# Two graph layers and two expert layers on one core: first query tile split during the edge count, spread by transpose, the last expert store moved to SyncE, a record load delayed

## The chip, the cores and the metric

The kernel runs on one core of a Trainium2 chip. The core has TensorE (PE in the profile, with its weight loads as PEld), VectorE (DVE), ScalarE (ACT), GpSimd (POOL) and SyncE (SP), each with its own instruction stream, and sixteen DMA engines that serve all of them. SyncE starts its transfers through hardware queues (q1, hardware_dynamic), GpSimd through software queues whose descriptors it writes itself (q0, software_dynamic). The metric is the time of one execution on the device in microseconds (us), the median of several runs; lower is better.

## The reference

A node array `x` of 1250 x 512 goes through four residual layers. What matters here:

```python
n, q, k, v = 1250, h @ Wq, h @ Wk, h @ Wv               # layer 1: graph attention, 8 heads of 64
e = einsum('ehd,ehd->eh', k[src], q[dst]) / 8           # 20000 edges
attn = segment_softmax(e, dst)
a = segment_sum(attn[:, :, None] * v[src], dst)         # then Wo, layer norms, a small MLP
x = x + layer1(layernorm(x))

x = x + of                                              # layer 2: 8 experts, top 2, capacity 187
#   h = gelu(x_e @ w1[e] + b1[e]) (512 -> 2048);  out = h @ w2[e] + b2[e];  scattered back by weight

x0, x1 = node_feats @ W_up                              # layer 3: messages over the same edges
tpw = silu_mlp(edge_attr_8) @ W_mlp4                    # per edge weights
msg = segment_sum(products of tpw, x0[src], x1[src], edge_attr_4)   # then W_out

x = x + shared_ffn + bank_sp + bank_fq                  # layer 4: two top-1 banks of 8 experts
```

## The kernel before

The whole array `X` stays in SBUF as 10 tiles of 125 nodes. The program is a sequence of blocks. Every block gives each engine a stream of its own, and all engines meet in a barrier at its end, so the last engine to arrive sets the start of the next block. The order within a block is written by hand, with semaphores; there is no scheduler. The blocks in the order of time, with the stretch of the profile:

- `front` (0 to 233 us): edge records are put in order, and q, k, v are computed. q goes to a DRAM tensor `q_dram`.
- `count_edges` (233 to 345 us): builds a dense table `LA` of logarithms of edge counts, node by node. VectorE writes one-hot tiles (`ohD`, line 564, a comparison with two SBUF inputs; `ohS`, line 569), TensorE multiplies them into a ring of four PSUM regions (line 588), ScalarE takes the logarithm of a finished region (line 619) and clears it (line 624). GpSimd does nothing but "grants": for each of 98 groups it loads a number and waits until that group's region is free (lines 537 to 539). SyncE loads the records and then writes zeros into the inputs of the later expert layers (line 1469).
- `attend` (345 to 665 us): for 10 tiles of queries and 8 heads each, TensorE computes scores against all 1250 keys (line 707, `scores`), VectorE adds the mask and takes the maximum (line 791), ScalarE exponentiates (line 852), TensorE transposes the probabilities (line 716, `turn`; 10 transposes for a head), VectorE and ScalarE copy them, and TensorE multiplies by V (line 725, `values`). There is one score buffer, so scores of head n+1 start after the mask of head n. A query tile must first be split in two parts, upper and rest: SyncE loads `QF` (line 671, `stage`), GpSimd copies it into `QS` (line 693) and subtracts (line 695), and then releases `q_split` (line 698), for which the scores of head 0 wait (line 707). Once per tile the inverse sums `rz_wide` (125 x 512) are spread over the output's layout by four products with the identity (line 736, `spread_inverse`), and VectorE multiplies by them (line 810).
- `dense`, `place_choices` (665 to 908 us): layer norms, MLP, routing of tokens to experts.
- `experts0` (908 to 1278 us): 8 experts one after the other. The rows of an expert (188 x 512) are turned back (line 1595) and copied by VectorE in two halves of 94 rows into `ye` (line 1677, counted by `back_moved`). GpSimd then stores both halves with one transfer of 94 x 2 x 512 (line 1562) and waits for it. `recycle` follows: GpSimd clears the used semaphores (line 100) between two barriers.
- `messages` (1278 to 1722 us) begins with `send_rows`: GpSimd gathers for each of 10 tiles the two expert rows of every node (line 1713, 20 gathers into a ring of 8 buffers `got`), VectorE adds them to `X` (line 1781, counted by `added`) and computes the moments; ScalarE normalises, TensorE transposes and multiplies, and SyncE stores the rows to `up_dram` (line 1707). Between the tiles (`between(t)`) VectorE does other preparations: it clears `MSG` (20 blocks, four at once, lines 1963 and 1967), converts the edge records (line 1970, from `t` = 4 on), scales weights, and builds the first one-hots. SyncE loads `RECS` (1568 KB of edge records, line 1839) and weights at the beginning of the block. When all rows are in `up_dram`, the loop over 196 tiles of edges begins.
- `tail`, `experts1` (1722 to 2015 us): layer 4.

The constants: `TILES` = 10, `BLOCKS` = 20, `GROUPS` = 98, `EXPERTS` = 8, `HALF0` = 94, `ROWS0` = 188.

## Time and profile before

| what | value |
|---|---|
| median of 3 runs | 2013.15 us (2009.31, 2013.15, 2964.96) |
| the profiled execution | 2016.69 us, span of the core 2015.0 us, mean granted clock 0.923 |
| busy: PE, PEld, DVE, ACT, POOL | 1669.8, 1204.0, 972.8, 727.3, 570.0 us |
| DMA | 262.15 MB, mean 130 GB/s |

The span is the time from the first to the last instruction of the core; the execution's own time has 1.7 us more. One of the three runs is far above the other two and is an outlier; the median is not touched by it. PE is busy for 83% of the span, but this is a mean over stages with different limits. The chain of waits that the profile prints ends with the last instruction and reaches back only to 1813.75 us, into layer 4; none of the changed places lies on it. So each place has to be read in its own stretch of time.

### The profile page before, as it was taken

To read this page: it belongs to the slowest core of one execution; us is meant where nothing else is said; L and a number is where in the kernel's file an instruction comes from. 1 tells how busy PE (TensorE), PEld (TensorE's weight loads), DVE (VectorE), ACT (ScalarE), POOL (GpSimd) and SP (SyncE) were. 2 spreads that over 40 slices of the span, in tenths; PEclk is the share of its full clock that TensorE was granted. 3 is DMA by queue.
4 is the path that set the end of the run, shared out by engine and by line. 5 is a ranking of instruction groups with operands and counts; after the bars stand their busy time and mean duration, and the time that the engine had idled before them with its cause. 6 is when DMAs were issued, how large, how long until landed. Compare 5 with 4: busy or idle time off the path is not lost. (4 is left out here: it accounts for less than half of the span.)

```text
span 2015.0 us, 33411 instructions
## 1 busy us (share of the span) xinstructions
PE 1669.8 (83%) x10239; PEld 1204.0 (60%) x10240; DVE 972.8 (48%) x1983; ACT 727.3 (36%) x1707; POOL 570.0 (28%) x656
## 2 busy tenths in 40 slices
PE   1990165999999697897999999179999999898992
PEld 1540032788888465557999999155555555646661
DVE  9210297666666475340000000358888888441232
ACT  1220053555555233441122211145555555422330
POOL 4777400110110121240000000435555554133132
PEclk9995599899999897897999999559999999998996
DMA  6200360110100601546777650545555555539983
GB/s 171 58 7 6 134 253 10 31 22 11 20 10 1 152 2 64 191 142 215 241 227 227 191 178 9 131 135 167 155 156 157 155 154 142 199 91 326 289 247 128
DMA packets 140526, 262.15 MB, mean 130 GB/s; under 512 B 41715, under 2 KB 59479, under 8 KB 135961
## 3 DMA queue, kind: packets, MB, share of 16 engines
q1 hardware_dynamic: 92792, 175.23, 27.8%
q0 software_dynamic: 47648, 85.82, 15.0%
q8 instruction: 50, 0.82, 0.2%
q14 instruction: 36, 0.29, 0.1%
HBM read 203.48 MB, written 57.38 MB: 129 GB/s over the span
## 5 line engine op out<-in xcount | busy, mean ns | idle before, releaser
L1891 PE MATMUL acc<-prod,ohy 128*64 128x256 f32 x1176 | 276.9, 385 | 8.3 <-DVE prod L2004 8.2
L1936 ACT ACTIVATE ohy<-oh,RECS 128x64 f32<-128x64 f32 x784 | 208.1, 336 | 168.6 <-PE acc L1891 168.6
L1891 PEld LDWEIGHTS acc<-prod,ohy 128*64 128x64 f32 x1176 | 153.8, 137 | 147.8 <-issue 83.3
L1868 POOL DMA_INDIRECT rows<-up_dram,idx x196 | 185.7, 947 | 172.3 <-DVE prod L2004 144.4
L1894 PE MATMUL acc<-prod,ohy 128*64 128x256 f32 x784 | 200.8, 394 | 0.0
L2004 DVE TENSOR_TENSOR prod<-w_ps,rows 128x768 f32<-128x768 f32 x196 | 185.7, 947 | 0.0
L244 POOL DMA_INDIRECT rec_dram<-recs,pos x157 | 154.5, 984 | 69.8 <-issue 48.9
L1672 DVE TENSOR_SCALAR FT<-y_ps,b2T 128x188 f32<-128x188 f32 x32 | 13.2, 413 | 328.8 <-PE y_ps L1621 328.8
L1609 PE MATMUL hid_ps<-FT,W 128*128 128x188 f32 x1024 | 168.5, 326 | 0.7 <-ACT FT L1646 0.7
L588 PE MATMUL ps<-ohS,ohD 128*128 128x512 f16 (+1 forms) x392 | 70.0, 305 | 118.6 <-DVE ohS L569 115.5
L1609 PEld LDWEIGHTS hid_ps<-FT,W 128*128 128x128 f32 x1024 | 166.1, 193 | 0.9 <-issue 0.9
L1621 PE MATMUL y_ps<-hid,W 128*128 128x188 f32 x1024 | 164.5, 323 | 0.0
L1621 PEld LDWEIGHTS y_ps<-hid,W 128*128 128x128 f32 x1024 | 162.9, 190 | 0.0
L791 DVE CUSTOM_DVE_ANT_0 S<-score_ps,LA 125x1250 f32<-125x1250 f32 x80 | 116.7, 1459 | 87.2 <-PE score_ps L707 86.3
L852 ACT ACTIVATE S<-S,mx 125x1250 f32<-125x1250 f32 x80 | 107.2, 1340 | 127.4 <-DVE mx L796 127.4
L588 PEld LDWEIGHTS ps<-ohS,ohD 128*128 128x128 f16 x392 | 33.8, 99 | 155.3 <-issue 151.2
L707 PE MATMUL score_ps<-KT,QS 128*125 128x512 f32 (+1 forms) x480 | 113.8, 373 | 12.3 <-POOLq L698 10.6
L2003 DVE TENSOR_TENSOR prod<-w_ps,rows 128x256 f32<-128x256 f32 x196 | 82.3, 420 | 70.4 <-PE acc L1891 54.0
L1562 POOL DMA_DIRECT2D yout<-ye x8 | 13.5, 1690 | 355.4 <-DVE ye L1677 355.4
L1884 PE MATMUL w_ps<-W,h 64*128 64x512 f32 x392 | 111.1, 644 | 0.0
L716 PE MATMUL turn_ps<-ident,S 125*125 125x125 f32 x800 | 108.4, 283 | 1.3 <-ACT PT L857 1.2
L725 PE MATMUL out_ps<-PT,V 125*64 125x125 f32 x1600 | 103.0, 274 | 1.5
(373 smaller groups left out, 2725.3 us busy)
## 6 DMA issues: line engine op xcount, KB each, us to landing
W<-in_L_ffn_w SPq DMA_DIRECT2D x16, 4096.0 KB, 23.4
bankW_sp<-in_L_ffn_W_sp SPq DMA_DIRECT2D x2, 4096.0 KB, 24.6
xin<-zeros SPq DMA_DIRECT2D x31, 256.0 KB
h_dram<-h3e SPq DMA_DIRECT2D x24, 256.0 KB, 4.5
h<-h_dram SPq DMA_DIRECT2D x24, 256.0 KB, 2.7
QF<-q_dram SPq DMA_DIRECT2D x20, 250.0 KB, 4.3
xin_sp<-zeros SPq DMA_DIRECT2D x18, 256.0 KB
xin_fq<-zeros SPq DMA_DIRECT2D x18, 256.0 KB
```

The lines of the kernel that those rows point to most:

```text
L244: pool.indirect_dma_start(out=rec_dram, out_offset=bass.IndirectOffsetOnAxis(ap=pos[0:rows_of, c:c + 1], axis=0), in_=recs[0:rows_of, c, : ...
L707: last = nc.tensor.matmul(score_ps[:P, c0:c0 + cn], QS[par][:, part, h, 0:P], KT[:, h, c0:c0 + cn], start=part == 0, stop=part == 1)
L716: last = nc.tensor.transpose(turn_ps[:P, 128 * s:128 * s + P], S[:, h % 2, P * s:P * (s + 1)], ident[:P, :P])
L791: nc.vector.tensor_tensor_reduce(out=S[:, h % 2, :], in0=score_ps[:P, 0:NODES], in1=LA[:, 2 * pairs - 2 + par, :], scale=1.0, scalar=-3e38 ...
L1609: last = nc.tensor.matmul(hid_ps[:, m % 4, 0:ROWS0], W1[b][:, k, 128 * m:128 * (m + 1)], xT[:, k, :], start=k == 0, stop=k == KC - 1)
L1621: last = nc.tensor.matmul(y_ps[:, d % 2, 0:ROWS0], W2[b][:, m, 128 * d:128 * (d + 1)], hid[:, m, :], start=m == 0, stop=m == MC0 - 1)
L1868: pool.indirect_dma_start(out=rows[:, t, :], out_offset=None, in_=up_dram, in_offset=bass.IndirectOffsetOnAxis(ap=idx[:, par, t:t + 1], ax ...
L1884: last = nc.tensor.matmul(w_ps[:, 2 * (pair % 2) + half, :], h3[mine, par, 128 * pair:128 * (pair + 1)], W4[mine, :], start=True, stop=True)
L1891: upper = lambda m: nc.tensor.matmul(acc[0:HALFB, bank, :].rearrange("p (b c) -> p b c", c=MUL)[:, m:4:3 - m, :], ohs[:, 1 + m, :], pr[:, ...
L1894: lower = lambda q: nc.tensor.matmul(acc[HALFB:128, bank, 256 * q:256 * (q + 1)], ohs[:, 0, :], pr[:, 0:3:2, :] if q == 0 else pr[:, 3:5, ...
L1936: last = nc.scalar.activation(ohy[:, t % OHY, i, :], oh[:, par, t, :], ACT.Copy, scale=RECS[:, bass.ds(BATCH * g + t, 1), 4 + i])
L2004: nc.vector.tensor_tensor(pr[:, 2:8, :].rearrange("p (a m) c -> p a m c", a=2), w[:, 2:4, :].unsqueeze(2).to_broadcast([128, 2, 3, MUL]), ...
```

## The change

Four edits, in four places.

1. **Query tiles.** `QF`, `QS`, their semaphores and the two programs `stage` (SyncE) and `split` (GpSimd) move out of `attend` into a new function `query_tiles`, called ahead of `count_edges`. SyncE loads query tile 0 behind the record load of `count_edges`, and GpSimd splits it after its last grant. `attend` starts with tile 1 on both engines. What each tile waits for is otherwise unchanged.
2. **Spreading the inverse sums.** The four products with the identity become four transposes.
3. **Last expert's store.** Expert 7's rows are no longer stored by GpSimd but by SyncE, in two halves of 94 x 512, each as soon as VectorE has copied it; SyncE waits for both. GpSimd stores experts 0 to 6 as before.
4. **Records.** SyncE loads `RECS`, the message weights and the first hidden chunks only after the first tile of `X` has got its two expert rows. VectorE clears 12 blocks of `MSG` before the first tile and 4 blocks after each of the tiles 0 and 1, instead of 4 before and 4 after each of the tiles 0 to 3.

```diff
+        def query_tiles(stack):
...
+            def stage(sp, i):
+                if not isinstance(i, int) or i > 0:
+                    sp.wait_ge(upper_ready, 2 * i)
+                    sp.sem_inc(tick, 1)
+                for half in range(2):
+                    sp.dma_start(QF[DK * half:DK * (half + 1)], q_dram[:, :, bass.ds(i * P, P)]).then_inc(q_loaded, 16)
+
+            def split(pool, i, par):
+                pool.wait_ge(q_loaded, 32 * (i + 1))
+                if not isinstance(i, int):
+                    pool.wait_ge(tiles_scored, i - 1)
+                    pool.sem_inc(tick, 1)
+                nc.gpsimd.tensor_copy(QS[par][:, 0, :, 0:P], QF[:]).then_inc(upper_ready, 1)
+                pool.wait_ge(upper_ready, 2 * i + 1)
+                nc.gpsimd.tensor_tensor(QS[par][:, 1, :, 0:P], QF[:], QS[par][:, 0, :, 0:P].bitcast(F32),
+                                        ALU.subtract).then_inc(upper_ready, 1)
+                pool.wait_ge(upper_ready, 2 * i + 2)
+                pool.sem_inc(q_split[par], 1)
...
                         sp.dma_start(RECS[:], rec_dram.rearrange("(p c) w -> p c w", p=128)).then_inc(loaded, 16)
-
+                        stage(sp, 0)
                         zeros_in = fill_zeros(sp, xin0, zeroed)
...
                         groups(pool, grant)
+                        split(pool, 0, 0)
...
-                        sp.sem_inc(upper_ready, 1)
-                        for par in range(2):
-                            stage(par, par)
-                        with sp.Fori(0, TILES // 2 - 1) as r:
+                        stage(sp, 1)
+                        with sp.Fori(1, TILES // 2) as r:
                             for par in range(2):
-
-                                stage(2 * r + 2 + par, par)
+                                stage(sp, 2 * r + par)
...
-                                last = nc.tensor.matmul(out_ps[:, 1 - par, P * q:P * (q + 1)],
-                                                        rz_wide[:, 2 * q:2 * q + 2, :].rearrange("p h c -> p (h c)"),
-                                                        ident[:P, :P], start=True, stop=True)
+                                last = nc.tensor.transpose(out_ps[:, 1 - par, P * q:P * (q + 1)],
+                                                           rz_wide[:, 2 * q:2 * q + 2, :].rearrange("p h c -> p (h c)"),
+                                                           ident[:P, :P])
...
+                        last = EXPERTS - 1
+                        for c in range(2):
+                            sp.wait_ge(back_moved, 2 * last + c + 3)
+                            sp.dma_start(yout0[last * ROWS0 + HALF0 * c:last * ROWS0 + HALF0 * (c + 1), :],
+                                         ye[last % 2][:, c, :]).then_inc(last_stored, 16)
+                        sp.wait_ge(last_stored, 32)
...
-                        with pool.Fori(0, EXPERTS // 2) as r:
+                        with pool.Fori(0, EXPERTS // 2 - 1) as r:
                             for b in range(2):
...
+                                store(r, b)
+                        store(EXPERTS // 2 - 1, 0)
...
+            def first_added(sp):
+                sp.wait_ge(added, per_tile)
...
                         load_mix(sp)
+                        first_added(sp)
                         sp.dma_start(RECS[:], rec_dram.rearrange("(p c) w -> p c w", p=128)).then_inc(recs_loaded, 16)
...
-                        CLEAR = 4
+                        CLEAR, FIRST = 4, 12
+                        nc.vector.memset(MSG[:, 0:FIRST, :], 0.0)
                         nc.vector.memset(acc[:], 0.0)
-                        nc.vector.memset(MSG[:, 0:CLEAR, :], 0.0)
 
                         def between(t):
-                            if t < BLOCKS // CLEAR - 1:
-                                nc.vector.memset(MSG[:, CLEAR * (t + 1):CLEAR * (t + 2), :], 0.0).then_inc(cleared, 1)
+                            if t < (BLOCKS - FIRST) // CLEAR:
+                                nc.vector.memset(MSG[:, FIRST + CLEAR * t:FIRST + CLEAR * (t + 1), :], 0.0).then_inc(cleared, 1)
```

How the instructions stand on GpSimd at the end of `count_edges` and the start of `attend`. The loads of `turnI` are the last grants, and `QS` is the split query tile. Before:

```order
L537 TENSOR_LOAD turnI
L537 ISA x2
L537 TENSOR_LOAD turnI
L537 ISA x2
L520 UNCONDITIONAL_BRANCH
L682 UNCONDITIONAL_BRANCH
L686 UNCONDITIONAL_BRANCH
L686 ISA
L693 CAST QS<-QF 128x8x125
L694 REGISTER_ALU
L695 TENSOR_TENSOR QS<-QF,QS 128x8x125
```

After the change:

```order
L566 TENSOR_LOAD turnI
L566 ISA x2
L566 TENSOR_LOAD turnI
L566 ISA x2
L514 CAST QS<-QF 128x8x125
L516 TENSOR_TENSOR QS<-QF,QS 128x8x125
L549 UNCONDITIONAL_BRANCH
L697 UNCONDITIONAL_BRANCH
L514 CAST QS<-QF 128x8x125
L516 TENSOR_TENSOR QS<-QF,QS 128x8x125
```

The first split stands ahead of the block's end (the branch of line 549), right behind the last grant; the second split is the first work of `attend`.

How they stand on SyncE at the end of `experts0` and the start of `messages`. Before:

```order
L1544 COMPARE_AND_BRANCH
L1525 UNCONDITIONAL_BRANCH
L1836 UNCONDITIONAL_BRANCH
L1701 DMA Wup<-in_L_gnn_W_up 128x128
L1702 DMA Wup<-in_L_gnn_W_up 128x128
L1839 DMA RECS<-rec_dram 128x3136
L1841 DMA W<-in_L_gnn_W_mlp 64x512 x2
```

After the change:

```order
L1549 COMPARE_AND_BRANCH
L1562 DMA yout<-ye 94x512 x2
L1530 UNCONDITIONAL_BRANCH
L1854 UNCONDITIONAL_BRANCH
L1716 DMA Wup<-in_L_gnn_W_up 128x128
L1717 DMA Wup<-in_L_gnn_W_up 128x128
L1858 DMA RECS<-rec_dram 128x3136
L1860 DMA W<-in_L_gnn_W_mlp 64x512 x2
```

The two half stores are the last work of SyncE in `experts0`. The record load keeps its place in the row, but a wait now stands between it and the loads of `Wup`.

On VectorE at the start of `messages`, before:

```order
L1962 MEMSET acc 128x1024
L1963 MEMSET MSG 128x2048
L1781 SCALAR_TENSOR_TENSOR X<-got,weight,X 125x512 x2
L1785 BN_STATS st_2<-X 125x6
L1786 BN_AGGR mv<-st_2 125x2
L1967 MEMSET MSG 128x2048
```

After the change:

```order
L1981 MEMSET MSG 128x6144
L1982 MEMSET acc 128x1024
L1799 SCALAR_TENSOR_TENSOR X<-got,weight,X 125x512 x2
L1803 BN_STATS st_2<-X 125x6
L1804 BN_AGGR mv<-st_2 125x2
L1986 MEMSET MSG 128x2048
```

The clear ahead of the first rows is three times as long, and two of the four clears between the tiles are gone further down.

## Rows read from the trace of the kernel before

**Rows 1.** Timeline: start us, us, engine, line, instruction [idle before <- releaser], count to attend
```profile
345.27 18.36 SPq L671 DMA_DIRECT2D QF<-q_dram  x6
350.42 1.02 POOL L693 CAST QS<-QF 128x1000 fp32r<-128x1000 f32 x1 [116.62 <-DMA QF<-q_dram]
351.53 2.12 POOL L695 TENSOR_TENSOR QS<-QF,QS 128x1000 fp32r<-128x1000 f32 x1
...
353.76 2.47 PE L707 MATMUL score_ps<-KT,QS 128*125 128x512 f32 x6 [10.57 <-POOLq L698]
...
357.94 2.47 PE L707 MATMUL score_ps<-KT,QS 128*125 128x512 f32 x6 [1.71 <-DVE mx L791]
```
**Rows 2.** Windows: us, busy (x) of PE, PEld, DVE, ACT, POOL, PEclk, DMA share, GB/s
```profile
305.00:325.00 20.00, 14.67 (x85) 7.06 (x84) 19.53 (x64) 10.34 (x13) 0.00 (x0) 1.00 0.00 0
...
346.00:347.00 1.00, 0.00 (x0) 0.00 (x0) 0.63 (x1) 0.42 (x1) 0.00 (x0) 0.83 0.28 38
...
366.00:372.00 6.00, 5.08 (x43) 4.24 (x43) 3.92 (x7) 4.22 (x6) 0.00 (x0) 1.00 0.04 6
```
**Rows 3.** One line, the grants: ns min/median/max, first and last start us
```profile
L539 POOLq EVENT_SEMAPHORE  x98: 17/17/17, 234.4 to 330.0; - x98
```
**Rows 4.** Timeline of place_choices: the GpSimd cast beside DVE L1347
```profile
797.19 2.26 POOL L1320 CAST ohT<-zeros 40x2500 fp32r<-40x2500 f32 x1
```
**Rows 5.** One line, DVE L1347: ns min/median/max of its two instructions
```profile
L1347 DVE TENSOR_TENSOR oh<-count,idxF x2: 243/1242/2242, 797.3 to 799.6; 125x80 f32<-125x80 f32 x2
```
**Rows 6.** Timeline of attend at the end of a tile: TensorE
```profile
397.75 0.97 PEld L736 LDWEIGHTS out_ps<-ident,rz_wide 125*128 125x128 f32 x8 [0.17 <-issue]
...
398.64 1.17 PEld L716 LDWEIGHTS turn_ps<-ident,S 125*125 125x125 f32 x10
...
399.76 1.37 PE L707 MATMUL score_ps<-KT,QS 128*125 128x512 f32 x6
```
**Rows 7.** Timeline: end of experts0, start of messages and its first tiles
```profile
1262.22 1.28 DVE L1677 COPY ye<-turn_ps 94x512 f32<-94x512 f32 x2 [0.73 <-PE turn_ps L1595]
1264.38 1.67 POOL L1562 DMA_DIRECT2D yout<-ye  x1 [38.18 <-DVE ye L1677]
...
1279.59 0.42 SPq L1839 DMA_DIRECT2D RECS<-rec_dram  x1
1279.74 1.28 POOL L1713 DMA_INDIRECT got<-yout,slot_out  x1 [0.82 <-issue]
...
1280.33 1.76 DVE L1963 MEMSET MSG<- 128x2048 f32 x1 [0.42 <-issue]
...
1293.74 0.75 DVE L1781 SCALAR_TENSOR_TENSOR X<-got,weight,X 125x512 f32<-125x512 f32 x1 [1.30 <-DMA got<-yout,slot_out]
...
1297.72 1.61 DVE L1781 SCALAR_TENSOR_TENSOR X<-got,weight,X 125x512 f32<-125x512 f32 x2
...
1302.55 1.60 DVE L1781 SCALAR_TENSOR_TENSOR X<-got,weight,X 125x512 f32<-125x512 f32 x2
...
1322.56 1.61 DVE L1781 SCALAR_TENSOR_TENSOR X<-got,weight,X 125x512 f32<-125x512 f32 x2
...
1326.14 1.60 DVE L1781 SCALAR_TENSOR_TENSOR X<-got,weight,X 125x512 f32<-125x512 f32 x2
```
**Rows 8.** Windows while the last expert's rows are stored, columns as in Rows 2
```profile
1272.00:1273.00 1.00, 0.00 (x0) 0.00 (x0) 0.00 (x0) 0.00 (x0) 0.00 (x0) 0.50 0.12 49
...
1276.00:1277.00 1.00, 0.00 (x0) 0.00 (x0) 0.00 (x0) 0.00 (x0) 0.00 (x0) 0.50 0.00 0
```
**Rows 9.** Timeline: a SyncE transfer of 94 x 2 x 512 and who waits for it
```profile
908.75 1.10 SPq L1528 DMA_DIRECT2D xe<-xin  x2
...
918.66 1.51 PE L1584 MATMUL turn_ps<-ident,xe 94*128 94x94 f32 x8 [9.16 <-DMA xe<-xin]
```
**Rows 10.** Timeline of layer 4: a first gather with no record load beside it
```profile
1979.63 1.25 POOL L2453 DMA_INDIRECT xe<-yout_fq,slots  x1 [2.67 <-DMA yout_fq<-FT]
...
1985.20 0.75 DVE L2564 SCALAR_TENSOR_TENSOR X<-xe,top_of,X 125x512 f32<-125x512 f32 x1 [9.08 <-DMA xe<-yout_fq,slots]
```

More of the change, by code:

```diff
@@ L492, in turning, with count_edges @@
             return pe_part, act_part
-        def count_edges(LA):
+        def query_tiles(stack):
+            sb = tile_in(stack)
+            QF = sb("QF", [128, HEADS, P])
+            QS = [sb(f"QS{par}", [128, 2, HEADS, 128], F32R) for par in range(2)]
+            q_loaded, upper_ready, tiles_scored, tick = sems_in(stack)("q_loaded", "q_upper_ready", "tiles_scored", "query_tick")
+            q_split = sems_in(stack)("q_split0", "q_split1")
+            def stage(sp, i):
[15 more added lines that the diff above has]
+                pool.sem_inc(q_split[par], 1)
+            return QS, tiles_scored, q_split, stage, split
+        def count_edges(LA, stage, split):
             HALFN = NODES // 2
@@ L625, in _, with attend @@
                                                      ACT.Copy).then_inc(evicted, 1)
-        def attend(KT, V, LA, T):
+        def attend(KT, V, LA, T, QS, tiles_scored, q_split, stage, split):
             with ExitStack() as st:
@@ L634, in attend @@
                 spread, lifted, deepened = sems_in(st)("inverse_spread", "values_lifted", "mask_deepened")
-                QF = sb("QF", [128, HEADS, P])
-                QS = [sb(f"QS{par}", [128, 2, HEADS, 128], F32R) for par in range(2)]
-                q_loaded, upper_ready, tiles_scored = sems_in(st)("q_loaded", "q_upper_ready", "tiles_scored")
-                q_split = sems_in(st)("q_split0", "q_split1")
                 S = sb("S", [P, 2, NODES])
@@ L665, in _ @@
                     def _(sp):
[L666 to L677 removed]
+                        stage(sp, 1)
+                        with sp.Fori(1, TILES // 2) as r:
                             for par in range(2):
[L680 removed]
+                                stage(sp, 2 * r + par)
                     @block.gpsimd
                     def _(pool):
[L685 to L686 removed]
+                        split(pool, 1, 1)
+                        with pool.Fori(1, TILES // 2) as r:
                             for par in range(2):
[L688 to L698 removed]
+                                split(pool, 2 * r + par, par)
                     @block.tensor
@@ L1510, in experts0 @@
                 stored = sems_in(st)("stored0", "stored1")
+                (last_stored,) = sems_in(st)("last_stored")
                 (b_turned, b_ready, x_turned, x_moved, hid_done, hid_moved, y_done, y_moved, back_done,
@@ L1791, in on_dve @@
                                                        in1=rstd[:, t:t + 1], op0=ALU.mult, op1=ALU.mult).then_inc(scaled, 1)
-            return load, store, fetch, all_stored, on_pe, on_act, on_dve
+            return load, first_added, store, fetch, all_stored, on_pe, on_act, on_dve
         def messages(MSG, picks):
@@ L2601, in gnn_moe_gnn_moe @@
             LA = sb1("LA", [P, TILES, NODES])
-            count_edges(LA)
-            attend(KT, V, LA, FT)
+            QS, tiles_scored, q_split, stage, split = query_tiles(attention)
+            count_edges(LA, stage, split)
+            attend(KT, V, LA, FT, QS, tiles_scored, q_split, stage, split)
         with ExitStack() as moe:
```

34 lines of the change are left out of this document (9 added, 25 removed).

## The prediction

> **What bounds the kernel now.** The page's chain of waits covers only the last 200 us, in layer 4, which the change leaves alone. I therefore read the timeline at each of the four places, and the windows for TensorE's granted clock. The question at each place is which event ends the wait last.
>
> At the start of attention it is the query tile. All engines come out of the barrier by 345.27, when SyncE issues the load of `QF`; GpSimd copies (1.02 us) and subtracts until 353.65; TensorE starts at 353.76 and had been idle for 10.57 us [rows 1]. In that gap its clock fell from full (2.4 GHz) to half (1.2 GHz): the mean of 346 to 347 is 0.83 [rows 2]. So the first scores take 2.47 us [rows 1] where a later head's take 1.37 [rows 6]. In the middle of attention TensorE goes from one group of matmuls to the next with gaps of 0.17 us at most [rows 6]: it is the bound there. In the count it is VectorE, busy 19.53 of 20 us, with TensorE at 14.67 [rows 2].
>
> At the end of the experts it is one transfer: VectorE is done at 1263.50, GpSimd issues at 1264.38 and needs 1.67 us for that [rows 7], and the data move at 49 GB/s until just before 1276.1, with a DMA share of 0.12 of sixteen engines, so two of them [rows 8]. At the start of `messages` it is the first gathers: issued at 1279.74, just after the 1568 KB record load of 1279.59; the second sum of tile 0 starts only at 1293.74 [rows 7].
>
> **Part 1, query tile 0.** Its load and split leave the start of attention. Load: two transfers behind the record load; the zero fills behind them are over by 305 (DMA share 0.00 [rows 2]) and the count lasts until 345, so the delay of these fills costs nothing. The split: the last grant is at 330.0 [rows 3], so GpSimd splits from 330.1 to 333.3, long before the barrier. TensorE can then start at about 345.3: **8.5 us** earlier, if the count ends as before.
>
> It won't quite. GpSimd computes beside VectorE here for the first time. A VectorE comparison with two SBUF inputs took 2.242 us while a GpSimd cast of 2.26 us ran, and its twin right after it 0.243 [rows 4, 5]: it waited for the cast. `ohD` is such a comparison. `ohS` has one SBUF input, and I don't know whether it waits too. GpSimd holds on for 1.02 + 2.12 = 3.14 us [rows 1]. If both kinds wait, VectorE, which has no slack, loses 3.1 us; if the two `ohS` of a group (about 0.3 us each, from 19.53 us over 64 instructions [rows 2]) run on beside each of the two GpSimd instructions, 3.1 - 2 x 0.6 = 1.9; if nothing waits, 0. I take 2.6, between the first two, since the instruction of rows 5 is the very kind of `ohD`. The Trainium skill (SBUF — State Buffer, "Who interferes with whom") says the same as a rule: a VectorE instruction with two SBUF inputs and a GpSimd instruction that reads SBUF exclude each other for their whole length; by it `ohD` waits and a one-port `ohS` does not, which would make the loss 1.9. By that rule, the trace agrees for `ohD`. Gain of the start: 8.5 - 2.6 = **5.9**.
>
> The clock: TensorE's pause becomes 2 us, and in the old trace the clock was still full 3 us after TensorE's last work (it fell inside 346 to 347). So attention should start at full clock. The first heads form a chain, because there is one score buffer: scores, mask, scores; the second scores came 4.18 us after the first [rows 1], of which 2.47 - 1.37 = 1.1 us was the half clock. Two such steps and a bit, as clock is full from 366 on [rows 2]: **2.3 us**. Tile 1 is now loaded at 345.3 and split by 353.7; it is wanted only 8 heads later, more than 20 us: nothing.
>
> **Part 2, transposes.** The four products stand as 8 passes and take 398.64 - 397.75 = 0.89 us; ten transposes of the same 125 x 125 take 399.76 - 398.64 = 1.12, 0.11 each [rows 6]. Four then take 0.45. TensorE is the bound, so 0.44 x 10 tiles = **4.5 us**. The bound from below is 2.0: on some tiles the next copy of ScalarE may be what TensorE then waits for.
>
> **Part 3, last store.** The first half can be issued at 1262.95 and the second at 1263.6, instead of both at 1264.38 by GpSimd. The nearest row for SyncE's part is the load of the same 94 x 2 x 512 to `xe`, issued at 908.75 and there at 918.66 [rows 9]: 9.9 us, no quicker than GpSimd's 11.7 (1264.38 to 1276.1) but for the issue. So half sizes don't halve the time: I let both together take 9.9 us from the first issue, and they land at 1272.8 instead of 1276.1, **3.3 us** earlier. By the Trainium skill (DMA: Bandwidth & Descriptors, "Why a DMA increments its semaphore by 16 and not by 1") the number of engines is the largest divisor up to 16 of the outer sizes, so 94 rows get two, and SyncE's transfers use the lowest ones; both halves would then share the same two, which is what I assumed. If they use different ones, 4 us more are gained. GpSimd also reaches the barrier early and settles there while the store runs, for which I add 0.7: **4.0**. Bounds: 2.5 and 8.
>
> **Part 4, records.** Without the load of 1568 KB beside them, gathers land as in layer 4, where the first took 1979.63 to 1985.20, 5.6 us [rows 10]. A first gather issued at 1279.74 lands at 1285.3; the second, issued after 1.28 us of GpSimd's work [rows 7] and a short gap, at about 1287.4 with a little more queueing, instead of 1293.74: **6.3 us**. Ahead of them VectorE now clears three times 2048 columns at 1.76 us each [rows 7] and `acc` (half a clear's columns, so 0.9 us), from 1279.0 to 1285.2: hidden by the first gather, at the edge. A tile with a clear takes 1302.55 - 1297.72 = 4.83 us, one without 1326.14 - 1322.56 = 3.58 [rows 7]; two tiles lose their clear: **2.5 us**. The records are issued when the second sum is done, about 1288, take some 8 us and are wanted by tile 4, about 1304 on this scale. They now collide with the gathers of tiles 2 and 3; a gather beside the records took up to 14 us from issue (1279.74 to 1293.74 spans two), but these have 8 to 10 us. I take off 0.5: **8.3**. Bounds: 2.5 (tiles 2 and 3 wait for what tile 0 waited for) and 8.8. GpSimd's 20 gathers, 1.28 us [rows 7] and a gap each, so about 1.5, end by 1310, ahead of tile 9 at 1320.
>
> **Sum.** 5.9 + 2.3 + 4.5 + 4.0 + 8.3 = 25.0 us. Span 2015.0 - 25.0 = 1990.0, that execution 1991.7. It was 3.5 us above the median of the runs, so the median becomes 2013.15 - 25.0 = **1988 us**, 1.2% less. A measurement of this kernel can tell about 2% (40 us) from no change, so this would be within.
>
> **Rivals.**
> - *The parts are worth less (12 in 100).* Each is hidden or eaten by the next wait: part 1 at 8.5 - 3.1 = 5.4 with no clock gain, part 2 at 2.0, part 3 at 2.5, part 4 at 2.5. Sum 12.4, time 2001. For it: the tight places named above, in part 4 above all. Against it: they'd all have to fall out badly.
> - *VectorE isn't held up and the half stores run side by side (15 in 100).* 8.5 + 2.3 + 4.5 + 8 + 8.8 = 32.1, time 1981. Against the first half stands rows 5.
> - *Slower: transposes let the clock fall (3 in 100).* If transposes don't count as work for the clock and attention fell to half clock, TensorE's time for a tile would grow by nearly its own length, about 8 x 3.6 = 29 us. One tile eats the whole gain, so from two tiles on it's slower: 1988 + 2 x 29 = 2046. The Trainium skill (TensorE: Matmul & The Clock Gate, "Part 4: PE-mode transpose") has that rule. Against it: ten transposes already stand in every head and the clock is 1.00 [rows 2]; the change adds 0.45 us of them to a tile of 29 and takes away 0.89 of matmuls.
> - *The change doesn't do what it says (5 in 100):* the grants are late or the load of tile 0 lands late and TensorE starts at 353 as before: 25.0 - 8.2 = 16.8, time 1996. Against it: fifteen us lie between the last grant and the barrier.
>
> The forecast itself has 65 in 100, with 1983 to 1994. The whole range reaches from 1977, the second rival less 4 us for the runs' spread (2009.31 against 2013.15), to 2002, the first rival. Faster by over 2% would need 40 us, more than all upper bounds together: 0.01. Slower by over 2%: the clock rival: 0.03.
>
> **What would show it.** Part 1: a GpSimd copy of `QF` at about 330; there, single `ohD` of 1 to 2 us instead of 0.4, the last `ohS` 2 to 3 us later, then first scores of 1.4 us within 3 us of the last count matmul. Part 2: 4 instead of 8 passes per tile, and a tile 0.44 us shorter. Part 3: two SyncE transfers at 1263 (shifted by the parts above), landing about 9 us later, and 12 us from VectorE's last copy to the first gather instead of 16. Part 4: second sum 8 us after the first gather's issue instead of 14, tiles 2 and 3 at 3.6 us, no wait for the records. I'm wrong if tiles 2 to 4 wait for gathers or records, or if the end of the count moves by less than 1 us or more than 4.

## The result, and the profile after

The changed kernel takes 1991.8 us, median of 4 runs (1988.5 to 1993.5); the kernel before took 2011.8 beside it, or 2010.4 without the outlier of 2965 us that is one of its 4 runs. The ratio is 0.9895 (95% interval 0.9883 to 0.9908): 1.05% or some 20 us less, clear of the noise but within the 2% that count as no change. The profiled spans are 2015.0 and 1991.8 us. The prediction said 1988, range 1977 to 2002. The time lies in the range, but the gain is some 20 us and not 25.

To compare places I count every trace from the start of the count block (GpSimd's first instruction there): what lies ahead of it is unchanged. `before`, `after`, `before_again`, `spread_by_matmul` and `fill_and_last_rows` ran on chips that reach the count after 233 us (kernel before: 2012 to 2015 us). The others ran on two chips, one for each of their sets, that reach it 76 to 89 us later and take 5 to 9 us more in the loop of `messages` (kernel before: 2105 and 2103 us); I call them the late chips. The columns are the starts of the first scores and of the last value product, the end of VectorE's last copy in `experts0`, the starts of the first gather and of the first index copy in `messages`, and the end of the program; the last three columns are differences.

| kernel | scores | values | last copy | gather | idx | end | values - scores | gather - copy | idx - gather |
|---|---|---|---|---|---|---|---|---|---|
| before | 120.7 | 430.2 | 1030.4 | 1046.7 | 1110.4 | 1781.9 | 309.5 | 16.2 | 63.7 |
| before_again | 121.0 | 430.0 | 1027.5 | 1043.8 | 1107.7 | 1776.9 | 309.0 | 16.2 | 64.0 |
| after | 113.8 | 418.9 | 1018.6 | 1031.0 | 1091.4 | 1758.9 | 305.1 | 12.4 | 60.3 |
| after_again | 114.1 | 417.8 | 1016.7 | 1029.1 | 1090.0 | 1764.8 | 303.7 | 12.4 | 60.9 |
| queries_as_before | 121.3 | 425.7 | 1022.9 | 1035.3 | 1096.1 | 1771.6 | 304.4 | 12.4 | 60.7 |
| spread_by_matmul | 114.5 | 422.5 | 1025.6 | 1038.0 | 1097.8 | 1765.6 | 308.0 | 12.4 | 59.8 |
| split_at_head | 120.6 | 425.5 | 1021.1 | 1033.5 | 1094.8 | 1770.8 | 304.9 | 12.4 | 61.3 |
| split_on_vector | 112.3 | 416.1 | 1016.0 | 1028.5 | 1089.4 | 1766.0 | 303.9 | 12.4 | 60.9 |
| records_late | 113.7 | 417.5 | 1018.8 | 1031.3 | 1091.0 | 1767.9 | 303.9 | 12.4 | 59.7 |
| records_early | 113.7 | 417.7 | 1019.1 | 1031.6 | 1086.9 | 1766.2 | 303.9 | 12.4 | 55.3 |
| store_80_14 | 113.9 | 418.2 | 1015.2 | 1020.7 | 1080.7 | 1756.6 | 304.3 | 5.5 | 60.0 |
| all_three | 112.5 | 417.4 | 1018.7 | 1024.3 | 1079.4 | 1752.7 | 304.9 | 5.6 | 55.1 |
| fill_and_last_rows | 112.9 | 416.1 | 1013.6 | 1019.2 | 1072.5 | 1745.2 | 303.2 | 5.5 | 53.4 |

By places the change gives 6.9 us at the first scores, 4.4 to 5.3 in the attention, 3.8 at the store and 3.1 to 3.4 in the first part of `messages`: 18 to 19 together.

**The count and the start of attention.** Timeline of the changed kernel while GpSimd splits the first query tile beside VectorE's one-hots, and at the first scores:

```profile
328.47 1.44 DVE L599 TENSOR_SCALAR ohS<-nodes,halfS 128x625 f16<-128x625 f16 x2
328.64 1.09 POOL L514 CAST QS<-QF 128x1000 fp32r<-128x1000 f32 x1 [94.94 <-issue]
329.81 2.41 POOL L516 TENSOR_TENSOR QS<-QF,QS 128x1000 fp32r<-128x1000 f32 x1
329.83 0.41 DVE L594 TENSOR_TENSOR ohD<-nodes,key 128x256 f16<-128x256 f16 x1
330.16 2.54 DVE L599 TENSOR_SCALAR ohS<-nodes,halfS 128x625 f16<-128x625 f16 x2
...
332.95 0.66 DVE L599 TENSOR_SCALAR ohS<-nodes,halfS 128x625 f16<-128x625 f16 x2
333.18 1.13 PE L618 MATMUL ps<-ohS,ohD 128*128 128x512 f16 x3 [1.55 <-DVE ohS L599]
...
346.77 2.44 PE L711 MATMUL score_ps<-KT,QS 128*125 128x512 f32 x6 [2.16 <-PEq L549]
```

A pair of `ohS` takes 0.66 us, and 1.44 and 2.54 beside the two GpSimd instructions: 2.66 us lost. I call this the hold-up. The 10.57 us pause of [rows 1] is 2.16, yet the first scores take 2.44 us, at half clock. Windows of the changed kernel (columns as in [rows 2]) show two falls:

```profile
333.50:336.00 2.50, 2.10 (x9) 0.88 (x8) 2.50 (x9) 0.00 (x0) 0.00 (x0) 0.50 0.00 0
337.00:346.00 9.00, 5.82 (x36) 2.81 (x34) 5.82 (x20) 1.33 (x2) 0.00 (x0) 1.00 0.00 0
347.00:356.00 9.00, 7.29 (x24) 6.15 (x25) 4.88 (x8) 2.99 (x4) 3.16 (x2) 0.50 0.28 58
```

**Attention.** `rz` is made once a tile, so its first and last start give nine tiles: 268.4 us in the kernel before, 263.9 after, 0.50 us a tile. TensorE's line has 40 instead of 80 passes. First the kernel before, then the changed one, one tile name (count, ns min/median/max, first to last start):

```profile
L834 DVE RECIPROCAL rz<-z x10: 193/193/193, 391.8 to 660.2; 125x8 f32<-125x8 f32 x10
```
```profile
L838 DVE RECIPROCAL rz<-z x10: 191/193/193, 384.9 to 648.8; 125x8 f32<-125x8 f32 x10
L740 PE MATMUL out_ps<-ident,rz_wide x40: 270/270/326, 390.9 to 652.4; 125*128 125x125 f32 x40
```

**The last store and the first sums.** Timeline of the changed kernel, to compare with [rows 7]:

```profile
1250.29 1.28 DVE L1692 COPY ye<-turn_ps 94x512 f32<-94x512 f32 x2 [0.73 <-PE turn_ps L1610]
1251.01 0.87 SPq L1562 DMA_DIRECT2D yout<-ye  x2
...
1263.99 1.29 POOL L1731 DMA_INDIRECT got<-yout,slot_out  x1 [0.82 <-issue]
1264.31 5.18 DVE L1981 MEMSET MSG<- 128x6144 f32 x1 [12.73 <-issue]
...
1270.52 1.53 DVE L1799 SCALAR_TENSOR_TENSOR X<-got,weight,X 125x512 f32<-125x512 f32 x2
...
1283.33 0.75 DVE L1799 SCALAR_TENSOR_TENSOR X<-got,weight,X 125x512 f32<-125x512 f32 x1 [3.14 <-DMA got<-yout,slot_out]
1285.13 0.75 DVE L1799 SCALAR_TENSOR_TENSOR X<-got,weight,X 125x512 f32<-125x512 f32 x1 [1.05 <-DMA got<-yout,slot_out]
...
1290.79 0.75 DVE L1799 SCALAR_TENSOR_TENSOR X<-got,weight,X 125x512 f32<-125x512 f32 x1 [2.38 <-DMA got<-yout,slot_out]
```

The sums are the `SCALAR_TENSOR_TENSOR`, two for each tile. The second one of tile 0 starts some 7.3 us behind the first gather's issue, not 14.0, and no longer waits for a gather but for the clears. Then tiles 2 and 3 wait 3.14, 1.05 and 2.38 us for their gathers. While the two halves of the store run, the DMA engines move as little as in [rows 8]:

```profile
1256.00:1257.00 1.00, 0.00 (x0) 0.00 (x0) 0.00 (x0) 0.00 (x0) 0.00 (x0) 0.50 0.13 51
```

So the data take as long as before. In windows of 1 us the engines are busy from 1266 to 1276 in the kernel before and from 1251 to 1261 in the changed one, some 9 us in both; VectorE's last copy ended at 1263.50 and at 1251.57. What the change saved is the time between that copy and the data.

### The profile page after: what moved, and what is told of

Read it like the earlier page. It is cut to its first block and busy times, and to the rows that moved or that the text cites. A ratio compares the mean times of both kernels' runs of the same rounds, so it can differ in the third digit from the quotient of the medians.

```text
span 1991.8 us, 33311 instructions
## 1 busy us (share of the span) xinstructions
PE 1664.9 (84%) x10199; PEld 1197.0 (60%) x10200; DVE 975.4 (49%) x1981; ACT 726.3 (36%) x1707; POOL 569.2 (29%) x655
## 5 line engine op out<-in xcount | busy, mean ns | idle before, releaser
L720 PEld LDWEIGHTS turn_ps<-ident,S 125*125 125x125 f32 x800 | 94.4, 190 | 13.0 <-issue 11.2
```

The source lines that it names most:

```text
L720: last = nc.tensor.transpose(turn_ps[:P, 128 * s:128 * s + P], S[:, h % 2, P * s:P * (s + 1)], ident[:P, :P])
```

## The experiments

Each is the changed kernel with an edit, timed in 4 to 6 executions beside the kernel before, in three sets. `after_again` is the changed kernel itself, and `before_again` is the kernel before, in a single execution.

**queries_as_before**: the query code of the kernel before, the rest of the change kept.

> Undoes the first part alone: queries are loaded and split in the attention block as in the kernel before, the other three parts stay. My account: the three parts give 4.9 (transposes), 3.8 (store) and 3.3 us (records), 12.0 together, and the first part is worth 7. So this one lies 12 to 13.5 us below the kernel before and 7 above the changed kernel. If the parts lean on each other (an earlier start of the attention that is lost at a later wait, so that undoing it costs nothing), it lies as low as the changed kernel, 20 below. If the account is short of something that the traces don't show (their spans differ by 23), it lies 16 below.

Ratio 0.9921 (0.9900 to 0.9941), 15 us below the kernel before. First scores at 121.3, 7.2 behind `after_again`, where the kernel before has them; by the places the part is worth 7.2 us. The totals can't settle it: the changed kernel itself, in the next set and on another of the late chips, also had 0.9921, and the two intervals are 9 and 12 us wide. Behind the first scores the long pause costs nothing: values - scores is 304.4 here and 303.7 to 305.1 in the eight kernels that have the transposes and the short one.

**split_at_head**: the first split ahead of the count's grants.

```diff
+                        stage(sp, 0)
                         sp.dma_start(RECS[:], ...).then_inc(loaded, 16)
-                        stage(sp, 0)
...
+                        split(pool, 0, 0)
                         groups(pool, grant)
-                        split(pool, 0, 0)
```

> The changed kernel, with the first queries loaded ahead of the count's records and split by GpSimd ahead of the first grant, while VectorE still waits for the records (its first one-hot in the changed kernel starts at 241.36, 8.4 us after the block's start). Theory 1, the hold-up: in the changed kernel the two one-hots L599 beside the split took 1.44 and 2.54 instead of 0.66, together 2.65 us; here none of the last one-hots is longer than 0.7, and the first scores, which stood 113.8 us behind the start of the count, stand 111.1 to 111.5 behind it. Theory 2, the clock: TensorE's clock was half at 333.1 to 336.5, when the late one-hots left it gaps of 1.9 us, and half again at 346.7 to 357.0. If the second fall comes of the first gaps, both are gone here and the first score group takes 1.2 instead of 2.44 us, for 2 us more. Rival: the pause of 2.1 us between the blocks brings it down by itself, the first group still takes 2.4, and only the 2.6 come. Rival 2: the split now delays the first grants, the one-hots start up to 3 us later, and the gain is eaten. By theory 1 alone 2.6 us below the changed kernel (22.6 below the kernel before), with theory 2 another 2 to 2.3; by rival 2 no difference to the changed kernel.

Ratio 0.9941 (0.9921 to 0.9961). This is 13 us below the kernel before, where 20 (rival 2) to 25 were expected. No `ohS` is over 0.39 us, so the hold-up is gone with GpSimd's work beside it; but rival 2 holds, and more than it said: the last one-hot ends 116.3 us behind the start (109.8 to 110.6 with the change) and the scores come at 120.6. The clock's first fall, beside the hold-up, is gone, and the one at the first scores is not (they take 2.44 us): theory 2 fails. The records, now loaded second, let the first one-hot start 12.6 instead of 10.7 us behind the start, which is 1.9 of it. The grants, one line of this kernel, start 9.7 us behind the block's start (at 318.2) instead of 1.3 and take 94.5 us from the first to the last, as in the other traces (94.2 to 95.6):

```profile
L568 POOLq EVENT_SEMAPHORE  x98: 17/17/17, 327.9 to 422.4; - x98
...
  DVE ohD L594: 7.6, 20
```

VectorE waits for them 20 times, 7.6 us. GpSimd's head start over VectorE was slack that the count uses up.

**split_on_vector**: VectorE splits, behind its last one-hot.

```diff
-                        split(pool, 0, 0)
...
                         groups(dve, one_hots)
+                        split(dve, 0, 0, nc.vector)
```

> The changed kernel, with the first queries' cast and subtraction done by VectorE behind its last one-hot, not by GpSimd beside the last one-hots. Theory, the hold-up: VectorE is idle from its last one-hot (342.8) to the start of the attention (346.7), 3.9 us; a cast and a subtraction of 1000 columns take it 1 us each, so they are hidden behind the last count matmuls and the last logarithms; the one-hots L599 take 0.66 us throughout; last one-hot and first scores come 2.6 us sooner, 111.2 us behind the start of the count. The run before this one, split_at_head, moved the split ahead of GpSimd's grants and lost 6.4 us, since the grants of 0.97 us each then set the pace; here the grants keep their place. Clock: if the gaps of TensorE beside the hold-up are what brought its clock down at 346.7, the first score group takes 1.2 us instead of 2.44 and another 2 come; if the 2.1 us pause does, it still takes 2.4. Rival: the grants (last at 328.5 in the changed kernel) bind the last groups, the one-hots end at the same time with shorter instructions and longer waits, and nothing is gained; or VectorE's split is longer than 3.9 us and the scores wait for it. By the theory 2.6 us below the changed kernel, or 4.6 with the clock; by the rivals 0 or slower.

```profile
429.27 0.67 DVE L514 CAST QS<-QF 128x1000 fp32r<-128x1000 f32 x1
429.98 1.20 DVE L516 TENSOR_TENSOR QS<-QF,QS 128x1000 fp32r<-128x1000 f32 x1
...
433.70 1.93 PE L711 MATMUL score_ps<-KT,QS 128*125 128x512 f32 x6 [2.13 <-PEq L549]
```

This timeline shows the split over at 431.2, 2.5 us ahead of the first scores. The last one-hot ends at 107.9, 2.7 ahead of `after_again` (110.6); the first scores gain 1.8 of it (114.1 to 112.3). So the hold-up cost the end of the one-hots what it measured. With no gap of TensorE beside it the first fall of the clock is gone (1.00 in every microsecond of the last 20 ahead of the scores), the second is not: the gaps of the hold-up aren't what brings it. The time of the first scores (1.93 us here) is no sign of it, since in `after_again`, with the hold-up, they take 1.39 and the clock falls only 1.6 us behind their start. The ratio, 0.9923 (0.9897 to 0.9948), is that of `after_again`: 2 us are below what so few executions resolve.

**spread_by_matmul**: the transposes of part 2 back to products (`nc.tensor.matmul(..., start=True, stop=True)`).

> Undoes the second part alone: the four products with the identity (32-bit, two passes each) in place of the transposes. If my account holds, a tile of the attention takes 30.3 us instead of 29.8 and the last values come 4.5 to 5 us later behind the first scores (303.8 to 305.1 in the changed kernel, 309.5 in the kernel before); the kernel lies 4.5 to 5 us above the changed kernel, 11 to 15 below the kernel before. Rival: the spread is hidden beside VectorE and ScalarE and the shorter attention of the changed kernel comes of the earlier start: 0.

Ratio 0.9923 (0.9907 to 0.9938), 16 us below the kernel before, where the changed kernel was 20 below it on a like chip. Nine tiles take 268.3 us again (the line of `rz`, as above), 4.5 more than with the transposes. values - scores is 308.0, against 305.1 in the changed kernel's first trace and 303.7 in its second: 2.9 and 4.3 us. The account holds.

```profile
L838 DVE RECIPROCAL rz<-z x10: 194/194/194, 384.6 to 652.9; 125x8 f32<-125x8 f32 x10
```

**store_80_14**: each of the last two stores cut at row 80.

```diff
-                            sp.dma_start(yout0[last * ROWS0 + HALF0 * c:..., :], ye[last % 2][:, c, :]).then_inc(last_stored, 16)
-                        sp.wait_ge(last_stored, 32)
+                            for p0, p1 in ((0, 80), (80, HALF0)):
+                                sp.dma_start(yout0[last * ROWS0 + HALF0 * c + p0:..., :], ye[last % 2][p0:p1, c, :]).then_inc(last_stored, 16)
+                        sp.wait_ge(last_stored, 64)
```

> The changed kernel, with each of the last two stores (94 rows, outer size 94 = 2 x 47, seen on two DMA engines at some 50 GB/s, 10.1 us from the first issue to landing) cut in two, of 80 and of 14 rows. Theory, the number of engines follows the outer size: 80 rows go over 16 engines and 14 over 14, the rows land within 3 to 4 us of the first issue, and the first gather comes 6 to 7 us sooner after the last copy (12.4 us in the changed kernel, 5.5 to 6.5 here). Rival: the split by rows is no matter and a store of so many rows stays at two engines: same 10 us. Rival 2: four issues of some 0.6 us each on SyncE and their four landings cost what the engines bring: 2 to 3 us gained. By the theory 6.5 us below the changed kernel (26.5 below the kernel before), by the rivals 0 or 2.5.

Ratio 0.9878 (0.9858 to 0.9899), 27 us below the kernel before. The changed kernel had 15.8 in its own set. Timeline and two windows:

```profile
1323.36 1.28 DVE L1693 COPY ye<-turn_ps 94x512 f32<-94x512 f32 x2 [0.73 <-PE turn_ps L1611]
1324.08 1.68 SPq L1563 DMA_DIRECT2D yout<-ye  x4
...
1330.17 1.29 POOL L1732 DMA_INDIRECT got<-yout,slot_out  x1 [0.82 <-issue]
```
```profile
1326.00:1327.00 1.00, 0.00 (x0) 0.00 (x0) 0.00 (x0) 0.00 (x0) 0.00 (x0) 1.00 0.52 152
1327.00:1328.00 1.00, 0.00 (x0) 0.00 (x0) 0.00 (x0) 0.00 (x0) 0.00 (x0) 1.00 0.00 0
```

In the last microsecond of the stores the DMA engines move 152 GB/s instead of 51, and in the one before it 219 at a share of 0.78 instead of 0.13 (0.95 in its busiest half). All is over by 1327, and it is 5.5 us from the last copy to the first gather instead of 12.4: the theory's 6.9 us, in every kernel that has this edit. More transfers alone don't do it: the change's two halves stayed at 0.13.

**records_late**: records asked for after tile 2's sums, used after tile 6.

```diff
-                sp.wait_ge(added, per_tile)
+                sp.wait_ge(added, 3 * per_tile)
...
-                            elif t == BLOCKS // CLEAR - 1:
+                            elif t == BLOCKS // CLEAR + 1:
```

> The changed kernel, with the records asked for after the sums of tile 2 (not tile 0) and put to use after tile 6 (not tile 4), the two steps behind them after tiles 7 and 8. Theory, the collision moved: in the changed kernel the records' 1568 KB ran from 1273 to 1281.3 beside the gathers of tiles 2 and 3, whose sums waited 3.14, 1.05 and 2.38 us, and the gain of 6.7 us at tile 0's sum was 3.3 from tile 4 on. Here the first three waits shrink to 1 us or less together, later tiles have their gathers four tiles ahead and don't wait, and the tail of this stage is 3.4 us earlier relative to its first gather (up to 6 if all of the 6.6 us of waits are the records' doing). Rival: the gathers alone are that slow (20 of 1.3 us each on GpSimd's side), the waits stay, and the time is that of the changed kernel. Rival 2: the waits move on to the tiles whose gathers now meet the records, or the records are late at tile 6, and the stage ends within 1 us of the changed kernel's. By the theory 3.4 us below the changed kernel (23.4 below the kernel before), by the rivals 0 to 1.

Ratio 0.9901 (0.9879 to 0.9922), 20 us below the kernel before, where the theory wanted 23. By the places rival 2 holds: idx - gather is 59.7 (60.3 and 60.9 in the changed kernel), tiles 2 and 3 don't wait any more, tiles 5 to 7 do. The waits of VectorE in this stretch (total, times, longest us), first here, then in the changed kernel:

```profile
DVE X L1799 <- DMA got<-yout,slot_out: 6.5, 5, 2.3
```
```profile
DVE X L1799 <- DMA got<-yout,slot_out: 6.6, 3, 3.1
```

**records_early**: records loaded in the middle of the last expert, into columns of `FT` that nobody uses then.

```diff
+                        sp.wait_ge(hid_done, MC0 * last + MC0 // 2)
+                        sp.dma_start(RECS, rec_dram.rearrange("(p c) w -> p c w", p=128)).then_inc(records_in, 16)
...
-                        sp.dma_start(RECS[:], ...).then_inc(recs_loaded, 16)
```

> The changed kernel, with the message stage's records (1568 KB) loaded in the middle of the last expert, when the DMA engines move 0 to 8 GB/s, into a part of FT that nothing uses till the tail. In the two kernels with the load inside the stage (after tile 0's sum, after tile 2's sum) the sums waited 6.6 and 6.5 us for gathers, of tiles 2 and 3 in the one, of tiles 5 to 7 in the other. Theory, the bytes: the load takes its place from the gathers wherever it is in the stage; out of the stage it costs nothing, the waits fall to 2 us or less, and the copy of the indices comes 4.5 to 6.5 us sooner behind the first gather (60.3 us in the changed kernel, so 54 to 56). Rival: gathers and stores of rows (7.5 MB) are the bound by themselves, the waits stay with W4's and the hidden rows' loads, 0 to 1.5 us gained. Rival 2: the load in the last expert delays its weights or its last stores, 1 to 8 us lost there. By the theory 5.5 us below the changed kernel.

```profile
DVE X L1806 <- DMA got<-yout,slot_out: 1.4, 1, 1.4
```

The waits fall from 6.6 to 1.4 us and idx - gather from 60.9 (`after_again`) to 55.3: 5.5 us, as the theory of bytes has it. At both places inside the stage that were tried the load costs them. Ratio 0.9903 (0.9877 to 0.9929), 2 us below the changed kernel in its set, where 5.5 were due; the profiled execution lost 2.6 us between the last values and the last copy. Rival 2, that the load delays the last expert, isn't the reason: from the copy that ends the expert before to its own last copy it takes 39.9 us in all thirteen traces, and the gather follows the last copy by 12.4 as in `after_again`. The 2.6 us lie in unchanged code ahead of it.

**after_again**, the changed kernel on a late chip, and **before_again**.

> The changed kernel itself, beside which the other three of this set are read on the same chip. The count block and the attention stand as before: first scores 113.8 us behind the start of the count, first gather 12.4 us behind VectorE's last copy, first gather to the copy of the indices 60.3 us. If the difference to the kernel before is a matter of the chip, it is not 20 us here.

Ratio 0.9921 (0.9891 to 0.9950), 15.8 us.

> The kernel before, profiled once beside the others, since on this chip the changed kernel was 15.8 us (0.5 to 1.1%) below it and not 20 us (1.05%). Counted from the start of the count block, on the first chip: first scores 120.7, first gather of the messages 1046.7, first copy of indices 1110.4, last 1465.9, end 1781.5. If the account by places holds here too, the first scores stand 6.6 us, the first gather 17.5 us and the first copy of indices 20.3 us behind the changed kernel's (114.1, 1029.1, 1090.0). If the four parts are worth less on this chip, these differences are smaller; if what is missing lies in unchanged code behind them, the differences are these and the loop of messages or the tail differs.

It ran on a chip of the first kind, so it can't answer what the late ones do. But it gives the two kernels twice: first scores 120.7 and 121.0 against 113.8 and 114.1, gather - copy 16.2 twice against 12.4 twice, idx - gather 63.7 and 64.0 against 60.3 and 60.9. Parts 3 and 4 rest on these pairs, since neither was undone by itself. The stretch from the last values to the last copy, unchanged in all, takes 595.6 to 603.0 us over these thirteen traces, in no order with the edits: so single spans can't be compared closer than some 4 us either way, and the places can.

**all_three**: `split_on_vector`, `store_80_14` and `records_early` in one.

> The changed kernel with three edits at once: the first split on VectorE behind the last one-hot, the last stores cut in 80 and 14 rows, the records loaded in the last expert. Store alone was seen with 5.5 us from the last copy to the first gather (12.4 in the changed kernel). If the places don't lean on each other, the sum is 2.6 + 6.9 + 5.5 = 15 us below the changed kernel, 35 below the kernel before. If the earlier gathers only meet something else (the records land beside the stores, or the rows' way through the stage is bound by bytes), it is 9.5 to 12.

Ratio 0.9856 (0.9828 to 0.9884), 2074.7 against 2087.5 us: 12.8 less. By places: 1.6 at the scores, 6.9 at the store, 5.8 in `messages`, 14.3 together. The gains add up at the places, and the total has nearly all of them.

**fill_and_last_rows**: `all_three` with seven idle matmuls behind the count, and the last store of `up_dram` cut in 112 and 13 rows.

```diff
+                        pe.wait_ge(logged, 2 * (BLOCKS - 3))
+                        for _ in range(7):
+                            nc.tensor.matmul(ps[:, 0:512], ohD[:, 0, :], ohS[:, 0, 0:512], ...)
...
+                    for p0, p1 in ((0, 112), (112, P)) if t == TILES - 1 else ((0, P),):
```

> The kernel all_three with two edits at places far apart. First: seven matmuls of 512 columns on leftover one-hots fill most of the 2.13 us that TensorE idles between the last count matmul and the first scores; their sums are overwritten, nothing reads them. In all ten traces the granted clock goes to half 0 to 2 us behind the first scores (or ahead, in the kernels before with the longer pause) and stays there 6 to 10 us, also where VectorE was never held up. Theory 1, the pause does it: with the filling the clock stays 1.00 over the first 20 us of the attention, the first score group takes 1.2 to 1.4 us, and the last values come 1 to 3 us sooner behind the first scores (305 us in all_three). Theory 2, the attention's own gaps at its start (TensorE waits 0.8 to 1.7 us between its first groups) do it: the clock still falls some us behind the first scores, and 0 to 1 us is gained. Second: the last of the ten stores of 125 rows to up_dram, outer size 125 = 25 x 5, is cut in 112 and 13 rows. By the rule that the number of engines follows the outer size, 16 and 13 engines take it in place of 5, and the copy of the indices follows the last row's eviction by 2.5 to 3 us instead of 4.3. Rival: the 4.3 us are latency and the sums of tiles 8 and 9's stores, 0 gained. Together 1.5 to 4.5 us below all_three, 30 to 33 below the kernel before (28.6 for all_three on this chip).

**1979.1 us, ratio 0.9822 (0.9806 to 0.9837)**: 1.8% or 36 us below the kernel before, and the fastest of all by its median. 30 to 33 us were expected. The places give 3.0 of the 7.6 us below `all_three`, which ran on a late chip; the rest is not accounted for. Timeline and windows:

```profile
343.93 1.67 PE L635 MATMUL ps<-ohS,ohD 128*128 128x512 f16 x7
...
346.24 1.38 PE L715 MATMUL score_ps<-KT,QS 128*125 128x512 f32 x6 [0.64 <-PEq L549]
```
```profile
346.24:349.24 3.00, 1.38 (x6) 1.00 (x6) 2.75 (x3) 1.09 (x1) 0.00 (x0) 1.00 0.59 122
351.00:353.00 2.00, 2.00 (x11) 1.91 (x10) 1.12 (x1) 0.00 (x0) 1.62 (x2) 0.53 0.00 0
355.00:360.00 5.00, 3.67 (x26) 3.30 (x26) 3.70 (x6) 2.91 (x4) 0.00 (x0) 1.00 0.52 102
```

By windows of 1 us the clock falls 3.2 us behind the first scores and is back 6.6 behind them; in `all_three` it falls 0.4 us ahead of them and is back 9.8 behind. values - scores is 303.2 against 304.9. So filling most of the pause (0.64 us of it are left) doesn't keep the clock up, as theory 1 wanted. That leaves theory 2, the spaced first heads, as the likelier one; no run changed their spacing, so it isn't shown. What the filling gained is open too: the changed kernel alone showed half clock for 10.2 us in one trace and 6.8 in the other, with 305.1 and 303.7, so 1.7 us is hardly more than that spread. The cut store is plain. In the timelines of `all_three` and then of this kernel the copy of the indices comes 4.29 us behind the last eviction's end (1395.76 + 0.60) and then 2.62:

```profile
1395.76 0.60 ACT L1791 ACTIVATE out_rows<-up_ps 125x512 f32<-125x512 f32 x1 [2.16 <-PE up_ps L1761]
1400.65 0.19 POOL L1885 COPY idx<-srcI 128x8 int32 x1 [22.62 <-DMA up_dram<-out_rows]
```
```profile
1302.70 0.60 ACT L1796 ACTIVATE out_rows<-up_ps 125x512 f32<-125x512 f32 x1 [2.16 <-PE up_ps L1766]
1305.92 0.19 POOL L1890 COPY idx<-srcI 128x8 int32 x1 [20.96 <-DMA up_dram<-out_rows]
```

## Why the prediction was right, and where it was not

**Part 1, start: 5.9 said, 6.9 found.** The pause shrank by 8.4 us (8.5 said) and the hold-up was 2.66 (2.6 said). The one-hots' end came only 1.9 later: they began 0.8 us later, behind a later landing of the records, but VectorE's waits for grants and free regions in the count were 1.3 us shorter (3.9 instead of 5.2). Neither was in my working, and the last count matmul ended only 1.5 later, which makes 8.4 - 1.5 = 6.9. *Who* waits was wrong: I bet on `ohD`, and `ohS` it was. So it is in part luck that 2.6 came out. In each pair one `ohS` lasts until just behind the end of the GpSimd instruction (329.73 and 332.22): 1.14 and 2.24 us, to 0.01, in all six traces with the split at this place. `ohD`, which came in between, took its usual 0.41 us, and GpSimd's subtraction beside it 2.41 us instead of 2.14, in all six too. So it looks as if each side waits for the other's instruction, whoever is first; that `ohD` is what stretches the subtraction was not tried by itself. The Trainium skill (SBUF — State Buffer, "Who interferes with whom") has both: besides instructions with two SBUF inputs it names `tensor_scalar` in a 2-port perf mode as one that takes the shared ports for its whole length. I read only the first half of it, and with it wrote that a one-input `ohS` doesn't wait; the measurement decides against my sentence and agrees with the page. That `ohS` runs in such a mode fits its 625 columns in 0.38 us, where `ohD` takes 0.42 for 256; no run shows the mode itself.

**The clock: 2.3 said, about 0 found.** The failed step is "So attention should start at full clock". In the nine traces with a short pause and no filling the clock was still full for most of the pause, and it fell between 0.5 us ahead of the first scores and 2.2 behind. It came back 7 to 10.2 us behind them (10.2 in the changed kernel's first trace), and 7.6 to 10.0 with the long pause. I had taken the end of the pause for the end of the danger; the first heads leave gaps of 1.7 us between groups, and filling the pause to 0.64 us didn't prevent the fall. What brings it stays open.

**Part 2: 4.5 said, 4.5 found** over nine tiles (0.50 each; 0.44 was said, which is 4.4 for ten tiles and not quite my 4.5), and 4.5 again when undone. The rival that transposes let the clock fall didn't come: it is 1.00 from 372 to 640 us in the changed kernel.

**Part 3: 4.0 said, 3.8 found.** Both halves together had a DMA share of 0.13 of sixteen, so two engines, at 51 GB/s. The Trainium skill (DMA: Bandwidth & Descriptors, "Why a DMA increments its semaphore by 16 and not by 1") makes the number of engines the largest divisor up to 16 of the outer size: 94 gives 2, 80 gives 16, 14 gives 14, 125 gives 5, 112 gives 16. By that rule, both cuts agree: the share of 0.13 became 0.78, and 4.29 us became 2.62.

**Part 4: 8.3 said, 3.3 found** (3.4 and 3.1 in the two pairs of traces). The mis-sized term is "I take off 0.5" for the records' meeting with the gathers of tiles 2 and 3. The second sum gained 6.7 (6.3 said), and the two saved clears came too, but 6.6 us of waits followed. `records_late` shows that they move when the load moves within the stage, `records_early` that without it idx - gather is 55.3, 8.4 less than before: about what I had forecast for the part, had nothing collided (8.8). My bounds had it (2.5 to 8.8); I took a slack of 8 to 10 us a gather for cover, though a gather beside the records had shown up to 14.

**The sum.** 6.9 + 0 + 4.5 + 3.8 + 3.3 = 18.5 at the places, 20 measured (18.5 to 23.5 by the interval), 15.8 on a late chip (10.5 to 23). Of the 6.5 us that the places are short of my 25, the clock is 2.3, the records 5.0 and the store 0.2, less 1.0 that the start gave more; so the range held because the start's surplus and the width of the range took up two terms that were wrong. What differs between places and totals lies within the spread of unchanged code. Which of that is chance of the execution and which of the chip stays open.

## What to carry to other kernels

- A big load that was moved inside a stage which lives on transfers picked other victims, at both places tried. Look for a stretch where the DMA engines idle (here the last expert: 9 GB/s on average from 1200 to 1249 us of the changed kernel) and a piece of SBUF that is free there.
- On a path that ends in one transfer look at its outer size first: cutting 94 rows in 80 and 14 gave 6.9 us, more than SyncE's queue, an earlier issue and halves together (3.8).
- Work that is moved into an engine's gap needs three questions: who shares its ports then, what queue it stands in (ahead of the grants the count ended some 6 us later), and whether the engine that waits for it hasn't got the gap itself (VectorE had 3.9 us and needed 1.9).

## What was not expected of the hardware

- A pair of one-input fp16 comparisons of 0.66 us took 1.44 and 2.54 beside GpSimd instructions of 1.09 and 2.41. GpSimd's subtraction took 2.41 with a two-input comparison of 0.41 at its start, and 2.14 without.
- TensorE's clock fell up to 2.2 us *after* work had begun again behind a pause of 2.1 us. The same kernel had 10.2 and 6.8 us of half clock there in two executions.
- VectorE does the split that takes GpSimd 1.02 + 2.14 us in 0.67 + 1.20.
